# Late key projections, key rotation inside the attention, and a new order of the weight-chunk loop

## The reference

```python
x = x + _L0_xattn_ref(_layernorm(x, axis=-1), ctx_4096, ...)   # fake_quant(x) @ fake_quant(ctx), 0..255
x = x + _L0_ffn_ref(_layernorm(x, axis=-1), w_gate, w_up, w_down)
x = x + _L1_xattn_ref(_layernorm(x, axis=-1), ctx_4096, ctx_4096, mask, wq, wk, wv, wo, 0)
x = x + _L1_ffn_ref(_layernorm(x, axis=-1), gate_w, up_w, down_w, gate_scale, up_scale, down_scale)

# _L0_ffn_ref: blocks of 32 share an exponent; x in fp6, weights in fp4
gate = _mx_linear(x, w_gate); up = _mx_linear(x, w_up)
return _mx_linear(silu(gate) * up, w_down)

# _L1_xattn_ref: 32 query heads, 8 key/value heads, 128 wide, 512 context rows for each of 2 batches
q = _apply_rope(query @ wq); k = _apply_rope(key @ wk); v = value @ wv
out = softmax(q @ k.T / sqrt(128) + mask) @ v   # four query heads share a key head
return out.reshape(...) @ wo
# _apply_rope(x) = x * cos + _rotate_half(x) * sin
```

## Time and profile before

| | before |
|---|---|
| median of 3 runs | 748.83 us |
| the profiled execution | 750.52 us |
| its span | 748.4 us |
| TensorE busy | 686.8 us, 3099 instructions |
| VectorE busy | 544.9 us |
| GpSimd busy | 431.5 us |
| ScalarE busy | 373.4 us |
| chain that ended last | 79% TensorE, 9% VectorE, 4% issue, 3% GpSimd |

### The profile page before, as it was taken

How to read it: one execution, slowest core, us unless ns; L and a number is a source line. 1 busy time by engine, 2 the same in 40 slices (tenths; PEclk the granted TensorE clock), 3 DMA queues, 4 the chain that set the end, 5 groups by cost and what they waited for, 6 DMA issues and landing times.

```text
span 748.4 us, 10869 instructions
## 1 busy us (share of the span) xinstructions
PE 686.8 (92%) x3099; PEld 502.1 (67%) x3104; DVE 544.9 (73%) x1054; ACT 373.4 (50%) x697; POOL 431.5 (58%) x387
## 2 busy tenths in 40 slices
PE   4698997997758999999999999999999999499998
PEld 1244443443336788888888888888888888388886
DVE  4877789957876788888788887888887895721113
ACT  1567533354234765666666566666665663111111
POOL 2465753741326776676766667676767453546672
PEclk9699998999989999999999999999999999799999
DMA  9943432122202121302122212112030112203221
GB/s 341 373 137 123 153 127 70 57 70 78 78 28 86 57 71 44 99 28 88 52 63 63 70 42 61 65 42 98 28 98 28 30 27 86 85 18 109 84 84 56
DMA packets 37162, 63.58 MB, mean 85 GB/s; under 512 B 3216, under 2 KB 11536, under 8 KB 36112
## 3 DMA queue, kind: packets, MB, share of 16 engines
q1 hardware_dynamic: 37136, 63.26, 25.7%
HBM read 53.81 MB, written 9.44 MB: 85 GB/s over the span
## 4 chain that ended last, share of the span: by engine, by line
PE 79%; DVE 9%; issue 4%; POOL 3%; ACT 2%; DMA 2%; SPq 1%; DVEq 0%; POOLq 0%; ACTq 0%
PE ps L539 16%; PE ps L541 16%; PE ps L540 16%; PE ps L601 11%; PE ps L568 7%; PE ps L447 5%; PE ps L455 5%; DMA idf<-in_ident 2%; PE ps L495 1%; DVE f L1138 1%; DVE f_amax L1133 1%; POOL k_swp L915 1%; DVE mx_amax L1095 1%; DVE f6c L1145 1%; POOL wq_sb L937 1%
## 5 line engine op out<-in xcount | busy, mean ns | idle before, releaser
L946 POOL TENSOR_SCALAR prob<-prob,rinv 128x512 f32<-128x512 f32 x128 | 89.0, 696 | 122.3 <-DVE rinv L1259 122.3
L810 ACT ACTIVATE prob<-ps,nmax 128x512 f32<-128x512 f32 x128 | 88.3, 690 | 61.8 <-DVE nmax L1252 59.5
L821 ACT CAST pT<-ps 128x512 fp32r<-128x512 f32 x128 | 75.1, 587 | 82.5 <-PE ps L568 81.6
L601 PE MATMUL ps<-xt,wq_sb 128*128 128x512 f32 x384 | 106.5, 403 | 5.2 <-POOL wq_sb L937 2.2
L1252 DVE CUSTOM_DVE_ANT_0 ps<-ps,mask_sb 128x512 f32<-128x512 f32 x128 | 88.3, 690 | 18.5 <-PE ps L541 17.5
L1273 DVE TENSOR_TENSOR pT<-ps,pT 128x512 fp32r<-128x512 f32 x128 | 86.8, 678 | 4.7 <-ACT pT L821 1.7
L601 PEld LDWEIGHTS ps<-xt,wq_sb 128*128 128x128 f32 x384 | 73.9, 194 | 24.0 <-issue 4.4
L568 PE MATMUL ps<-idf,prob 128*128 128x128 f32 x512 | 76.6, 272 | 0.0
L447 PE MATMUL ps<-ctxT,wk_sb 128*128 128x512 f32 x128 | 64.0, 657 | 12.0 <-DMA ctxT<-in_ctx_cols 9.9
L568 PEld LDWEIGHTS ps<-idf,prob 128*128 128x128 f32 x512 | 63.9, 141 | 16.2 <-POOL prob L946 0.3
L455 PE MATMUL ps<-wv_sb,ctxT 128*128 128x512 f32 x128 | 65.4, 658 | 7.2 <-DVE idb L1152 3.6
(11 more groups left out here) (148 smaller groups left out, 1614.8 us busy)
## 6 DMA issues: line engine op xcount, KB each, us to landing
mx_raw<-in_mxw SPq DMA_DIRECT2D x8, 1024.0 KB, 7.4
wq_raw<-in_wq SPq DMA_DIRECT2D x32, 256.0 KB, 3.2
wo_raw<-in_wo SPq DMA_DIRECT2D x32, 256.0 KB, 2.7
k_scr<-k_cos SPq DMA_DIRECT2D x16, 256.0 KB, 3.1
v_scr<-v_st SPq DMA_DIRECT2D x16, 256.0 KB, 2.7
kr<-k_scr SPq DMA_DIRECT2D x16, 256.0 KB, 2.8
vr<-v_scr SPq DMA_DIRECT2D x16, 256.0 KB, 3.9
ffn_raw<-in_gate_w SPq DMA_DIRECT2D x11, 256.0 KB, 2.7
```

The lines of the kernel that those rows point to most:

```text
L601: last = mm(query_bank(H), wq_sb[:, par, l, k], xt[:, r, k], start=(n == 0), stop=(n == 11))
L810: nc.scalar.activation(prob[:, j], bank(j % 2), ACT.Exp, bias=nmax[:, j:j + 1], scale=-1.0, accum_out=rsum[:, j:j + 1]).then_inc(exps, 1)
L821: copy(pT[:, v % 2, 0, :, i * P:(i + 1) * P], bank(2 + i % 2).rearrange("p (k c) -> p k c", k=4)).then_inc(ph_ready, 1)
L946: nc.gpsimd.tensor_scalar(prob[:, i], prob[:, i], rinv[:, i:i + 1], 1.0, ALU.mult, ALU.mult).then_inc(probs, 1)
```

## The change

It has five parts. (1) Of the 16 key units five, (5,1), (6,0), (6,1), (7,0) and (7,1), leave the chunk loop (`LATE_KEYS`) and are issued, whole or in halves, in the quantised feed-forward, among the row transposes, and behind the first queries. (2) Only the keys of head 0 are rotated in the loop. All others are copied out as they are (`copy_keys`) and rotated in the attention: the load brings a second, half-swapped copy (`kr_swp`), GpSimd multiplies it by the sine, VectorE multiplies `kr` by the cosine and adds. (3) The loop has a new table of units (`STEPS`), a new order of the first DMAs, the bf16 identity is cast by ScalarE, GpSimd scales the next chunk in before it scales the last one out, and VectorE takes the peaks before the clip. The read-out of the first attention, the layernorm and the fp6 quantisation stand one step later on VectorE. (4) At the end of the attention the last projection has another bank and the row statistics are taken earlier. (5) GpSimd starts the split of the second chunk of the last feed-forward only behind the layernorm. Buffers are laid out anew to suit; that part is left out here.

```diff
-ROW_BANKS = ([4, 5, 0, 1], [4, 5, 6, 7])
-L0_AT = 4
+ROW_BANKS = ([4, 5, 0, 7], [4, 5, 6, 7])
+STEPS = (
+    ([("v", 0, 0), ("v", 1, 0), ("v", 2, 0), ("v", 3, 0)], [("k", 0, 1)]),
+    ([("v", 0, 1), ("v", 1, 1)], [("k", 1, 0)]),
+    ([("k", 1, 1), ("v", 2, 1)], [("k", 2, 0)]),
+    ([("v", 3, 1), ("k", 2, 1)], [("v", 4, 0)]),
+    ([("v", 4, 1), ("k", 3, 0)], [("k", 3, 1)]),
+    ([("v", 5, 0), ("v", 5, 1)], [("k", 4, 0)]),
+    ([("k", 4, 1), ("v", 6, 0)], [("v", 6, 1)]),
+    ([("v", 7, 0), ("v", 7, 1)], [("k", 5, 0)]),
+)
+LATE_KEYS = ((5, 1), (6, 0), (6, 1), (7, 0), (7, 1))
+LATE_BANK = (3, 6, 2, 1, 3)
+VALUES = [unit[1:] for step in STEPS for part in step for unit in part if unit[0] == "v"]
+KEYS_AT = {1: 2, 3: 3, 4: 4, 5: 5}
+Q_AT, L0_AT = 1, 4
...
-                kv_store(i)
+                stores(STEPS[i][0] + STEPS[i][1])
+            k_load(6)
...
+                    if not first_keys(g):
+                        sp.dma_start(kr_swp[0:64, b], rows[64:128]).then_inc(kr_in[b], 16)
+                        sp.dma_start(kr_swp[64:128, b], rows[0:64]).then_inc(kr_in[b], 16)
...
+            k_load(7)
+            for i, b in LATE_KEYS[:4]:
+                key_store(i, b)
+            sp.wait_ge(ffn0_done, NT)
             for U in range(4):
                 unit(U, U, 0)
+                if U == 0:
+                    key_store(*LATE_KEYS[4])
...
+            keys(0, 0, 0)
             for i in range(NFULL):
-                keys(i, 0)
-                keys(i, 1)
-                if i == 0:
+                project_context(STEPS[i][0])
+                if i == 1:
                     pe.wait_ge(consts_ready, 2)
-                else:
+                    pe.wait_ge(k_roped, 1)
+                if i > 0:
                     mx_turn(i - 1, 0)
-                values(i, 0)
+                project_context(STEPS[i][1])
                 if i > 0:
                     mx_turn(i - 1, 1)
-                values(i, 1)
-                if i == 1:
+                if i == Q_AT:
...
+            def late_keys(n, parts):
+                i, b = LATE_KEYS[n]
+                if parts[0] == 0:
+                    pe.wait_ge(wk_in[i % 2], 16 * (i // 2 + 1))
+                    if n == 1:
+                        pe.wait_ge(inter_ready, 3 * NT)
+                    if n == 2:
+                        pe.wait_ge(ffn0_done, 3)
+                    if n == 3:
+                        pe.wait_ge(intT_ready, NT)
+                    if n == 4:
+                        pe.wait_ge(ffn0_done, 4)
+                key_part(i, b, LATE_BANK[n], parts)
...
             gate_up(0)
+            late_keys(0, range(0, 2))
             mx_turn(NFULL - 1, 0)
             mx_turn(NFULL - 1, 1)
             gate_up(1)
             mx_turn(NFULL, 0)
+            late_keys(0, range(2, 4))
             pe.wait_ge(mx_kept, 2 * NFULL + 1)
             turn_inter(0)
             for t in range(2, NT):
                 gate_up(t)
                 down(t - 2)
                 turn_inter(t - 1)
+            late_keys(1, range(0, 2))
             down(NT - 2)
+            late_keys(1, range(2, 4))
             turn_inter(NT - 1)
+            late_keys(2, range(0, 2))
             down(NT - 1)
+            late_keys(2, range(2, 4))
...
+                    if isinstance(U, int) and U in (-2, -1) and j == 3:
+                        late_keys(4, range(2 * U + 4, 2 * U + 6))
...
+            def copy_keys(i, b):
                 act.wait_ge(k_sums, 2 * i + b + 1)
-                after(act, k_roped, 2 * (i - 1) + b + 1)
-                n = rotating(("k", i, b))
+                slot = (2 * i + b) % NSLOT
+                after(act, k_stored[slot], 16 * (i // 2))
+                copy(k_st[:, slot], bank(key_bank(i, b))).then_inc(k_copied, 1)
...
+            swap(0)
             mx_lift(0, 0)
             mx_lift(0, 1)
+            act.wait_ge(id_in, 16)
+            copy(idb[:], idf[:]).then_inc(consts_ready, 1)
+            copy_values(0, 0)
             rows_scale()
-            for i in range(NFULL):
-                swap(i, 0)
+            copy_values(1, 0)
+            copy_values(2, 0)
+            mx_lift(1, 0)
+            copy_values(3, 0)
+            mx_lift(1, 1)
+            rows_keep()
+            swap(1)
+            for i in range(1, NFULL):
+                copy_unit(STEPS[i][0][0])
                 mx_lift(i + 1, 0)
-                swap(i, 1)
-                if i == 0:
-                    rows_keep()
-                if i >= 1:
-                    mx_keep(i - 1, 0)
+                copy_unit(STEPS[i][0][1])
                 if i + 1 < NFULL:
                     mx_lift(i + 1, 1)
-                copy_values(i, 0)
-                if i >= 1:
-                    mx_keep(i - 1, 1)
-                if i == 0:
+                mx_keep(i - 1, 0)
+                copy_unit(STEPS[i][1][0])
...
             scale_in(0)
+            pool.wait_ge(rk_in, 16)
+            key_sine(0)
             scale_in(1)
-            pool.wait_ge(rk_in, 16)
 
             for i in range(NFULL):
-                key_sine(i)
-                scale_out(i)
+                if i == 1:
+                    key_sine(1)
                 if i + 2 <= NFULL:
                     scale_in(i + 2)
-                if i == L0_AT + 1:
+                scale_out(i)
+                if i == L0_AT + 2:
...
+                    if j == 3 and u in (1, 2) and within(g + 1, NKV) and not first_keys(g + 1):
+                        b = u - 1
+                        pool.wait_ge(kr_in[b], 48 * g + 64)
+                        tt(kr_swp[:, b], kr_swp[:, b], ropeK[:, 1], ALU.mult).then_inc(key_sined, 1)
...
+            pool.wait_ge(ln_ready, 4 * NT)
...
+            mx_peaks(0)
             mx_exponents(0)
             quantise_rows()
+            mx_peaks(1)
             mx_exponents(1)
-            dve.wait_ge(rk_in, 16)
-            dve.wait_ge(id_in, 16)
-            nc.vector.tensor_copy(idb[:], idf[:]).then_inc(consts_ready, 1)
             for i in range(NFULL):
                 mx_round(i, 0)
-                key_cosine(i, 0)
+                if i < 2:
+                    key_cosine(i)
                 mx_round(i, 1)
+                if i < 2:
+                    key_rotate(i)
+                if i + 2 <= NFULL:
+                    mx_peaks(i + 2)
                 if i == 0:
                     clip_rows()
-                key_cosine(i, 1)
-                mx_clip(i)
-                key_rotate(i, 0)
-                key_rotate(i, 1)
-                if i + 2 <= NFULL:
-                    mx_exponents(i + 2)
-                if i == 1:
+                if i == 2:
+                    sum_rows()
                     clip_context(0)
-                    sum_rows()
-                if i == 2:
+                if i == 3:
                     clip_context(1)
-                if i == L0_AT - 1:
+                if i == L0_AT:
                     attention0(0)
-                if i == L0_AT:
+                if i == L0_AT + 1:
                     attention0(1)
                     dve.wait_ge(l0_done, NT)
                     layernorm()
-                if i == L0_AT + 1:
+                if i == L0_AT + 2:
                     dve.wait_ge(ln_ready, 2 * NT)
                     fp6(rows(xhat[:]), NT * D)
                     fp6_clip(NT * D, [])
+                mx_clip(i)
+                if i + 2 <= NFULL:
+                    mx_exponents(i + 2)
...
+                            row_stats(2)
+                            aggregate(2, 3)
                     if j == 3 and within(U - 2, NUNIT):
                         dve.wait_ge(oh_ready, U - 1)
                         tt(oT[:, u % 2, 1], bank(4 + u % 2), oT[:, u % 2, 0].bitcast(F32), ALU.subtract).then_inc(o_split, 1)
+                        if isinstance(U, int) and U == NUNIT + 1:
+                            dve.wait_ge(proj_added, 2 * NUNIT - 2)
+                            row_stats(0)
+                            row_stats(1)
+                            aggregate(0, 2)
...
+                    if (u, j) in ((1, 2), (2, 3)) and within(g + 1, NKV) and not first_keys(g + 1):
+                        b = u - 1
+                        dve.wait_ge(kr_in[b], 48 * g + 64)
+                        tt(kr[:, b], kr[:, b], ropeK[:, 0], ALU.mult).then_inc(key_cosed, 1)
+                    if (u, j) in ((2, 2), (3, 0)) and within(g + 1, NKV) and not first_keys(g + 1):
+                        b = u - 2
+                        dve.wait_ge(key_cosed, 2 * g + b + 1)
+                        dve.wait_ge(key_sined, 2 * g + b + 1)
+                        tt(kr[:, b], kr[:, b], kr_swp[:, b], ALU.add).then_inc(key_roped, 1)
```

233 lines of the change are left out of this document (153 added, 80 removed).

## The result

| | before | after |
|---|---|---|
| median (4 runs each) | 748.12 us | 721.10 us |
| ratio, 95% interval | | 0.9644 (0.9618 to 0.9670) |
| span of the profiled execution | 748.4 us | 718.7 us |
| first matmul of the quantised feed-forward | 167.01 | 130.91 |
| from there to the row transposes | 45.82 | 46.72 |

The change is faster by 27.0 us, 3.6%. Differences of those times give the gain by stage: 36.1 in the chunk loop, -0.9 in the quantised feed-forward, 2.2 more up to the attention, then **-10.7 inside the attention** (the lead falls from 37.44 to 26.75), and 3.0 at its end: 29.7 of span.

What follows compares the result with a forecast made beforehand. The loop was taken as bound by TensorE after a start without work, with VectorE's queue setting the new end. 748.4 - 35.0 + 1.0 - 1.6 + 1.5 - 3.0 = 711.3 span, told as 712 us; range 703 to 727.

Steps and rivals of the forecast that it cites:

- rival 2: Attention: three crowded VectorE instructions at 1.77 us each, 13 us in all instead of 1.5, time 723.5; 17%.
- three signs of being wrong: TensorE without gaps sets the loop's end; TensorE waits for the key's low part in attention; first gate matmul after 140 us.
- nine tenths: Chunk loop, profile after: VectorE busy at nine tenths or more.
- Loop, -35.0 forecast: Chunk loop: the first gate matmul starts at 132.0 instead of 167.0 us, -35.0.
- Walking VectorE's queue: Chunk loop: VectorE durations from 22.7 us to the exponents of chunk 8 sum to 92.2, plus 6 of waits.
- TensorE with gaps of one to four microseconds: Chunk loop, profile after: TensorE shows gaps of one to four microseconds.
- Rival 1: Chunk loop: the opening stays slow, only 17.5 us comes back instead of 35.0, time 729.5; 12%.
- Late keys, +1.0: Quantised feed-forward: three late key projections (10.3 us) mostly fit TensorE's idle time and cost 1.0 us; bounds 0 and 10.3.
- Start of the attention, -1.6: First queries: the fourth and fifth late keys keep TensorE's clock up, returning 1.6 us.
- Key rotation in the attention, +1.5: Attention: added VectorE and GpSimd key work costs 1.5 us over seven groups; bounds 0 and 44.4.
- the three crowded instructions: Third unit of an attention group: three added VectorE instructions, 2.8 us against about 2.2 of gaps and 1.0 of slack.
- End of the attention, -3.0: End of the attention: normalised rows at 645.1 instead of 648.06 us, -3.0; bounds -1.5 and -4.5.

Runs made afterwards that it cites:

- experiment 5: Kernel before, three of four matmuls of five key projections out: 0.9972; also without rotating keys of heads 1 to 7: 0.9889. Changed kernel, five value projections computed twice: 0.9785.
- experiment 6: Kernel of experiment 2 with old orders: VectorE's first attention read-out, layernorm and fp6 one step earlier, 727.05 us; GpSimd scaling out before in, 722.84.
- experiment 7: Changed kernel, first loads nearly in old order: 724.09 us; changed kernel, three of four late-key matmuls out: 722.93; kernel before, only the new attention end: 747.25.
- experiment 2: Changed kernel with VectorE's sum of the second key half moved behind the low part of the first half: 708.22 us (0.9448).

## Why the prediction was right, and where it was not

The forecast was 712, range 703 to 727; 721.1 came. Direction, range and the sum's large terms held, but the case that happened is in substance rival 2 (723.5), to which 17% was given. The span came out at 718.7, not 711.3: the key rotation cost 9.2 us more than its term, and the other terms together gave 1.8 more than theirs. The rest of the distance is how the profiled executions lay beside their medians.

Two of the prediction's three signs of being wrong came about: TensorE runs without gaps into the end of the loop, and it waits for the key's low part in every group. VectorE in the loop has 80.1 of 95 us, not nine tenths. That the time still lies in the range is due to its width and to the loop, not to the attention's term.

- *Loop, -35.0 forecast, -36.1 measured.* Walking VectorE's queue gave the right end. Its parts were less right: the exponents of chunk 8 ended at 117.7 instead of 120.9, and the fp6 rows then waited 1.8 us for TensorE's own queue. "TensorE with gaps of one to four microseconds" is true up to 93.8 and false after; there TensorE and VectorE are both all but full, and experiment 5 shows that more work on TensorE is mostly paid for. That the queue walk came out so well owes something to the order being the one it assumed: experiment 6 shows 16 and 10 us more in the loop on orders for which the same sum of durations would have given nearly the same time.
- *Rival 1, the loop loses only its five units, 17.5.* Its premise was wrong: in the old loop 13.1 us of TensorE were worth 1.5. And the opening did not stay slow: from 6.5 to 36 us the granted clock was 1.00, and 0.77 before.
- *Late keys, +1.0.* +0.9 by the two profiles, but the kernel with the old code and only the new tail has 46.87 us for this stage too, and experiment 7 gains nothing by leaving them out, so the cost is nought within that scatter.
- *Start of the attention, -1.6.* -2.2; 2.1 by experiment 7.
- *Key rotation in the attention, +1.5: the step that failed.* It measured +10.7, of which 8.3 are seven times 1.2, 1.7 the first group's third and fourth unit (1.1 of it stays without VectorE's key work), 0.7 the last units. The sum took the three crowded instructions at 0.94 us each, 2.8; they took 1.10, 0.93 and 1.82, together 3.85. Rival 2 had the dearer price, 1.77, for all three. What decides between them was in the trace of before: 0.54 us and what is left of GpSimd's instruction. The free time was taken too large as well: 2.2 us of gaps and 1.0 of slack, as if all could be spent; 3.85 us of work and 1.2 lost leave 2.6. The gaps lie before instructions that wait for TensorE or ScalarE, and a queue that is late once also delays ScalarE's exponential and behind it the high part of the query, which the key's low part stands behind. The share of busy time (45.4 of 52.3) says nothing of it: in experiment 2 it is 45.3 of 51.1, and no group after the first loses anything.
- *End of the attention, -3.0.* -3.0, in two kernels.

## What to carry to other kernels

An engine with an eighth of its time free can still be the bound for one microsecond a turn: when work is added to its queue, find the instruction that the critical engine waits for, and put the new ones behind it, but look at what the new place delays and at what GpSimd runs there; two moves by three tile steps were worth 9 us gained and 9 us lost here. Before counting on a released engine, ask which queue sets the pace, and where the freed one will stand next: removed work became a wait of 13.8 us. Work taken off TensorE was worth 1.5 us in the old loop, off TensorE and VectorE 10.7, and with the new opening and order 36; taking back one step of the order cost 10 or 16 us of the loop. And read the granted clock beside the busy time: some 10 of the 36 us are the same TensorE work at the higher clock.

## What was not expected of the hardware

A VectorE instruction of 0.20 us took 3.63, to the end of a GpSimd product of 3.64 that began just before it, seven times in a row (six on 64 elements a lane, the last on 16), while roundings with one input in PSUM kept their 1.22 us beside GpSimd's other product of 3.64, the scaling in. The Trainium skill ("SBUF — State Buffer", Who interferes with whom) says that whoever issues first holds the shared port pair for its whole instruction, and lists tensor_scalar among those that can ask for it; the trace agrees. VectorE instructions of 128x512 with both inputs in SBUF took 0.67 us once, when no GpSimd instruction ran at the start, and else 0.54 us plus what was left of GpSimd's instruction, 0.93, 1.09 or 1.82 in the places above. GpSimd pays as well: its key product took 1.73 us at 386.07, begun 0.36 us into a VectorE product, for the 1.29 of the query's.
